# A decoder layer on one core: the second group's projections moved into the first group's cross-attention end and third norm

## The reference

```python
x = x + attn(layernorm(x))            # linear attention with decay
x = x + xattn(layernorm(x), ctx)      # causal cross-attention, 16 heads
x = x + ffn(layernorm(x))             # 8 experts, top 2, plus a shared one

# attn
xx = shift(x) - x                     # the token before, minus this one
r, k, v = (x + xx*maa_r) @ Wr.T + br, (x + xx*maa_k) @ Wk.T + bk, (x + xx*maa_v) @ Wv.T + bv
g = silu((x + xx*maa_g) @ Wg.T + bg)
# per head: att = r @ k * decay matrix; y = att @ v (and a carried state)
y = groupnorm(y) * ln_g + ln_b
return (y * g) @ Wo.T + bo
# xattn
return softmax(causal(q @ k.T / 4)) @ v @ Wout.T
# ffn
combine = top-2 softmax weights of x @ router_w.T
return sum_e combine_e * ((silu(x @ w_gate_e) * (x @ w_up_e)) @ w_down_e) + sigmoid(x @ shared_gate_w) * shared
```

## Time and profile before

| | |
|---|---|
| three runs | 650.09, 653.31 (median), 655.36 us |
| profiled execution | 653.28 us, span 651.6 us |
| busy | PE 608.5 (93%), DVE 409.7 (63%), POOL 337.5 (52%), ACT 277.4 (43%) |

### The profile page before, as it was taken

One profiled execution on the slowest core, in us unless ns is written; L12 is line 12 of the kernel. 1 busy time (PEld: TensorE's weight loads), 2 busy tenths in 40 slices (PEclk: granted clock), 3 DMA queues, 4 the chain that ended last, 5 costly groups with the idle time before them and its releaser, 6 DMA issues.

```text
span 651.6 us, 15490 instructions
## 1 busy us (share of the span) xinstructions
PE 608.5 (93%) x6296; PEld 484.9 (74%) x6296; DVE 409.7 (63%) x840; ACT 277.4 (43%) x632; POOL 337.5 (52%) x456
## 2 busy tenths in 40 slices
PE   7987958699999999999999999998999999999996
PEld 6544546454888889854888888854798888899996
DVE  6797787859743755869753655879762655742120
ACT  4856322132335655351325555342325555343322
POOL 7674154014355666615355666524364566618666
PEclk9989998799999999999999999999999999999999
DMA  7921000002020112102021111102011112114220
GB/s 188 352 82 34 1 1 2 2 1 66 26 83 25 42 41 59 28 16 68 20 82 32 39 41 58 30 17 68 16 51 34 38 43 58 28 55 113 69 69 16
DMA packets 41824, 34.08 MB, mean 52 GB/s; under 512 B 9901, under 2 KB 41206, under 8 KB 41754
## 3 DMA queue, kind: packets, MB, share of 16 engines
q1 hardware_dynamic: 39850, 31.27, 17.2%
q10 hardware_dynamic: 1904, 1.84, 0.9%
HBM read 30.92 MB, written 2.17 MB: 51 GB/s over the span
## 4 chain that ended last, share of the span: by engine, by line
PE 36%; DVE 23%; POOL 17%; ACT 11%; issue 10%; DMA 2%; ACTq 0%; SPq 0%; POOLq 0%; DVEq 0%
PE bank L1014 7%; DVE A L1504 6%; DVE nm L1581 5%; POOL hb L620 4%; POOL A L695 3%; POOL hT_last L704 3%; PE bank L1196 3%; POOL hT L609 3%; ACT A L885 2%; PE bank L1123 2%; ACT L799 2%; PE bank L1011 2%; PE bank L1213 2%; PE bank L1112 2%; DVE hb L1479 2%
## 5 line engine op out<-in xcount | busy, mean ns | idle before, releaser
L609 POOL TENSOR_TENSOR hT<-hb,hT 128x256 fp32r<-128x256 f32 (+1 forms) x102 | 78.2, 767 | 73.0 <-ACT hT L768 73.0
L620 POOL TENSOR_TENSOR hb<-hb,cwb 128x256 f32<-128x256 f32 (+1 forms) x102 | 77.2, 757 | 71.1 <-DVE hb L1479 71.0
L1479 DVE TENSOR_TENSOR hb<-hb,bank 128x256 f32<-128x256 f32 (+1 forms) x102 | 42.7, 419 | 105.1 <-ACT hb L778 105.1
L768 ACT ACTIVATE hT<-hb 128x256 fp32r<-128x256 f32 (+1 forms) x102 | 42.4, 416 | 126.6 <-POOL hb L620 126.1
L1018 PE MATMUL bank<-xTf,wGh 128*128 128x256 f32 x272 | 82.9, 305 | 0.0
L1504 DVE TENSOR_TENSOR A<-bank,decay 128x512 f32<-128x512 f32 x128 | 77.4, 683 | 8.2 <-PE bank L1112 8.2
L1019 PE MATMUL bank<-xTf,wGh 128*128 128x256 f32 x272 | 76.7, 282 | 0.0
L1020 PE MATMUL bank<-xTf,wGl 128*128 128x256 f32 x272 | 76.6, 282 | 0.0
L1019 PE MATMUL bank<-xTf,wUh 128*128 128x256 f32 x256 | 72.2, 282 | 0.0
L1018 PE MATMUL bank<-xTf,wUh 128*128 128x256 f32 x256 | 72.1, 282 | 0.0
L1020 PE MATMUL bank<-xTf,wUl 128*128 128x256 f32 x256 | 72.0, 281 | 0.0
(11 more groups left out here) (221 smaller groups left out, 1424.3 us busy)
## 6 DMA issues: line engine op xcount, KB each, us to landing
cwb<-cw_rows SPq DMA_DIRECT2D x54, 128.0 KB, 2.9
A<-cw_rows SPq DMA_DIRECT2D x18, 128.0 KB, 3.4
A<-in_x SPq DMA_DIRECT2D x4, 512.0 KB, 4.1
res<-in_x SPq DMA_DIRECT2D x4, 512.0 KB, 4.4
out_x<-res SPq DMA_DIRECT2D x8, 256.0 KB, 2.4
rawG<-in_L_ffn_w_gate SPq DMA_DIRECT2D x2, 704.0 KB, 6.4
rawU<-in_L_ffn_w_up SPq DMA_DIRECT2D x2, 704.0 KB, 6.5
cwb<-cw_rows SPq DMA_DIRECT2D x12, 112.0 KB, 2.6
```

What stands on the lines that cost most here:

```text
L609: pool.tensor_tensor(hT[hr, c % 2, 1, :], hb[hr, c % 2, :], hT[hr, c % 2, 0, :].bitcast(F32), ALU.subtract).then_inc(h_lo, 1)
L620: pool.tensor_tensor(hb[hr, c % 2, :], hb[hr, c % 2, :], cwb[hr, c % CWS, :], ALU.mult).then_inc(h_scaled, 1)
L1479: tt(h, h, up_part(PS[5 + c % 2], n), ALU.mult).then_inc(gu_used, 1)
```

## The change

All of it is in group 0 and at the start of group 1.

- POOL: the low parts of pieces 0 to 2 stand behind the last receptance and not between receptances. The down pieces 4 to 7 are no longer shared between DVE and POOL; POOL does them whole, 4 and 5 at n5 (behind piece 3), 6 and 7 behind the masks of batch 3. The power for group 1's first norm stands behind the masks of batch 1, and the zeroed edge behind those of batch 2.
- DVE: no down pieces. Differences and the first two mixed inputs of group 1 stand before `attended(2)`, the next two behind `attended(3)`, the following two between statistics and application of the third norm.
- ACT: the copy of the turned input (`mixed_input(1)`) stands in the midst of the exponentials of batch 3; r and k are taken before the third norm, g in front of the router's exponential, with a load of the Exp table behind it.
- PE: the first norm of group 1 is turned before batch 2 is attended. `project` takes a list of halves: r before the output product of cross-attention, k and half of v behind it, the other half of v behind the third norm, g's halves around the router's transpose. r's halves go to banks 6 and 5. The transposes of the routing weights stand inside the first scores of group 1. 17 idle products in place of 22 before the second norm. The first half of the output product waits for three normalised batches and not four.

```diff
+        def r_bank(g, m):
+            return (6, 5)[m] if g == 1 else (4, 2)[m]
...
             if n < 7:
-                j0, j1 = FD[n - 4]
-                cut = j0 + 2 * (j1 - j0) // 3
-                w = slice(cut, j1) if pool_side else slice(j0, cut)
+                w = slice(*FD[n - 4])
...
-        LOW_AT = dict(n5=(1, 2, 3), x0a=(0, 4, 5), r2=(6, 7))
-        LOW_POOL_AT = dict(n5=(3,), x1c=(4,), x3c=(5, 6))
+        LOW_AT = dict(n5=(1, 2, 3), x0a=(0,))
+        LOW_POOL_AT = dict(n5=(3, 4, 5), x3c=(6, 7))
...
-                    elif g == 0 and u >= 5:
-                        split_low(u - 5)
-                if g == 0:
+                if g == 0:
+                    for n in range(3):
+                        split_low(n)
...
-                    if b == 0 and g + 1 < NG:
+                    if b == (0 if g else 1) and g + 1 < NG:
                         layer_rstd(0, g + 1)
-                    if b == GB - 1 and g + 1 < NG:
+                    if b == (GB - 1 if g else 2) and g + 1 < NG:
                         zero_edge(g + 1)
...
-                        exponentials(b + 1, range(4))
+                        exponentials(b + 1, (0, 1))
+                        if b == 2:
+                            mixed_input(1)
+                        exponentials(b + 1, (2, 3))
...
                 if g == 0:
-                    mixed_input(1)
+                    take_rk(1, 0)
+                    take_rk(1, 1)
...
-                if g + 1 < NG:
+                if g == 0:
+                    take_g(1)
+                    act.activation(spare, mhalf[:, 0:1], ACT.Exp).then_inc(exp_table, 1)
+                elif g + 1 < NG:
                     take_rk(g + 1, 1)
...
                         elif n == 5 and g:
+                            if g == 1:
+                                turn_routing(0)
                             pe.wait_ge(cwT_ready, g)
...
-                    idle_product(22, 7)
+                    idle_product(17, 7)
...
                         key_scores(b + 1)
+                        if b == 2:
+                            pe.wait_ge(p_exp, 12)
+                            turn_norm(0, 1, tokx, 2)
                         attend(b)
...
                 if g == 0:
-                    turn_norm(0, 1, tokx, 2)
+                    project(1, 0)
...
-                halves = 2 if g else 4
+                halves = 2 if g else 3
...
+                else:
+                    project(1, 1)
+                    project(1, 2, (0,))
                 turn_norm(2, g, tok2, 0)
...
+                else:
+                    project(1, 2, (1,))
...
-                if g + 1 < NG:
+                if g == 0:
+                    project(1, 3, (0,))
+                elif g + 1 < NG:
                     project(g + 1, 1)
...
-                if g + 1 < NG:
+                if g == 0:
+                    project(1, 3, (1,))
+                elif g + 1 < NG:
                     project(g + 1, 2)
                     project(g + 1, 3)
...
-                    layer_apply(0, g + 1, tokx, tokx)
-                    point(g, "x2a")
+                    layer_apply(0, 1, tokx, tokx)
+                    input_differences(1)
+                    mixed_input(1, 0)
+                    mixed_input(1, 1)
                     attended(2)
                     attended(3)
+                    mixed_input(1, 2)
+                    mixed_input(1, 3)
```

More of the change, by code:

```diff
@@ L1070, in point, with turn_routing @@
                         ffn_tick(g - 1, n)
+            def turn_routing(g):
+                pe.wait_ge(cw_ready, g + 1)
+                for b in range(GB):
+                    last = nc.tensor.transpose(PS[cw_bank(g)][0:E + 1, b * T:(b + 1) * T], cw[:, b, :], ident[:])
+                last.then_inc(cw_turned, 1)
             pe.wait_ge(ident_made, 1)
@@ L1344, in _ @@
                         gate_up(g, n)
[L1345 to L1351 removed]
+                if g:
+                    turn_routing(g)
+                else:
+                    pe.wait_ge(f_lo[0], len(FW))
+                    pe.wait_ge(f_lo[1], NFW)
             for n in range(4, AHEAD):
@@ L1678, in _ @@
                 if g + 1 < NG:
-                    for c in range(4, 8):
+                    for c in range(4 if g else 6, 8):
                         mixed_input(g + 1, c)
```

34 lines of the change are left out of this document (14 added, 20 removed).

## The result

The changed kernel took 659.31 us (median of 4 runs, 657.62 to 660.45) against 653.19 for the kernel before (4 runs, 650.09 to 655.36): ratio 1.0095, 95% interval 1.0048 to 1.0142. It is slower. Run again, against other runs of the kernel before (the fifth experiment), it gave 1.0128, 1.0095 to 1.0162. I had forecast no change that can be told, 654.0, and 647.3 to 658.5: the measured time lies above my range, near what my slower rival gave (660.2). The profiled execution took 659.61 us with a span of 657.9. All ratios in this document are those on record and not quotients of the two medians; that of experiment 8 leaves out the two slow ones of its ten runs (656.02 and 656.54 us), and the plain mean of all ten over that of the kernel before is 0.9987.

What follows compares the result with a forecast made beforehand. No engine was taken to bound the kernel; the chain passes between engines. +3.9 (second norm, both early gains included) - 3.1 - 0.1 gave +0.7 us, 654.0; own range 651.5 to 657, over all cases 647.3 to 658.5.

Steps and rivals of the forecast that it cites:

- rival 2: PE's new gaps bring half clock in attention, last half projection and decay products: 6.9 us slower, 660.2; chance 0.07.
- Split pieces behind the receptances: POOL, group 0: PE's wait for the last receptance goes, moved pieces cost nothing before the memsets; gain 1.0 us.
- Five idle products fewer: PE before the second norm: 17 idle products for 22 let the norm be turned earlier; gain 0.7 us.
- The queue at the second norm: DVE's and POOL's split pieces run one by one after X, the norm's last output; maxima 3.9 us later, early gains included.
- The first rival: Second norm: back-to-back DVE instructions go ahead of waiting POOL, first maxima at 79.6; 647.2 in all, chance 0.15.
- To the third maxima: First to third maxima: DVE pieces and the power leave, batch 1's masks come earlier; 16.4 instead of 19.5, gain 3.1 us.
- To the first decay product: Third maxima (m) to the second group's first decay product: new chain takes 44.7 instead of 44.8 us, gain 0.1.
- My own sign of being wrong: Router product to first decay product: prediction wrong if the routing takes much longer than 13 us.
- After it 32 of them follow at the same pace: Second group's decay products: after the first, 32 follow at the pace before the change, so its shift is the time's shift.

Runs made afterwards that it cites:

- the fifth experiment: The changed kernel itself, unaltered, run again against other runs of the kernel before on another chip: 660.02 us, ratio 1.0128.
- experiment 8: Changed kernel with POOL's pieces 4 and 5 behind batch 1's masks, router exponential before the Silu, last down pieces held until group 1's second mixed input: 651.37 us, 0.9968.
- experiment 10: Kernel before with two early edits alone, split pieces behind the receptances and 17 idle products for 22: 650.97 us, ratio 0.9986.
- experiment 1: Changed kernel with POOL's down pieces 4 and 5 moved from the second norm to behind the masks of batch 1: 653.22 us, ratio 1.0043.
- experiment 4: Kernel before with only the changed kernel's whole split pieces and their tables, POOL doing all down pieces: 655.68 us, ratio 1.0079.
- experiment 3: Changed kernel with 17 idle products on PE between the router's transpose and the last half projection: 657.96 us, ratio 1.0115.
- experiment 7: Changed kernel with 17 idle products in the routing, plus 9 before and 3 behind the turning of the routing weights: 656.87 us, ratio 1.0099.
- experiment 9: Kernel of experiment 8 plus idle products: 17 before the last half projection, 4 behind it, 3 behind the routing weights' turning: 648.30 us, ratio 0.9960.
- experiment 11: Kernel before, nothing moved, with 16 idle products behind cross-attention's output product, before the third norm is turned: 651.45 us, ratio 1.0015.
- experiment 6: Changed kernel with ACT's router exponential before the gate's Silu and no Exp table load behind it: 657.74 us, ratio 1.0104.
- experiment 12: Changed kernel with POOL's down pieces 6 and 7 held until group 1's second mixed input is made: 658.32 us, ratio 1.0132.

## Why the prediction was wrong

1. **Split pieces behind the receptances**, -1.0. The wait of PE went: the last 20 decay products of group 0 follow without a gap and the group norm starts 1.2 us earlier. But 0.7 of it was lost at once, on something I had costed at nothing: POOL's memsets, which had ended just before a DVE instruction that works from SBUF to SBUF, now met it. DVE in the changed kernel:

```profile
57.08 0.97 DVE L1550 TENSOR_SCALAR A<-A 128x128 int32<-128x128 int32 x1
...
58.08 0.23 DVE L1552 TENSOR_SCALAR A<-A 128x128 int32<-128x128 int32 x1
```

 The same kind of instruction took 0.97 and 0.23 us; the memsets run from 56.98 to 57.97 (POOL's first row above). In all eleven profiled executions with these pieces moved the first of the two takes 0.82 to 0.99 us beside the memsets, and in the three others 0.23. X came 0.5 us earlier (72.90) and not 1.0.

2. **Five idle products fewer**, -0.7. Measured 0.5 (7.87 to 7.34 in experiment 10).

3. **The queue at the second norm**, with both early gains +3.9. Right in mechanism, and measured +3.7: first maxima forecast at 85.15, measured 84.92; experiments 1 and 4 show it alone, both ways. That it fits to 0.2 us is partly luck: X came 0.5 later than forecast, and the queue took 12.0 from X instead of 12.75. The first rival (DVE keeps its turn) is out: DVE and POOL took turns. The row behind it, the receptance at 32.42 that came in only after several short DVE instructions, stays unexplained. The rule of the Trainium skill that I set against the change ("SBUF — State Buffer", section "Who interferes with whom": the second to issue blocks until the first is through) agrees with this case's trace: DVE's two pieces took 9.07 us, nearly the 3.2 of their own plus the 6.3 of POOL's two.

4. **To the third maxima**, -3.1. Here the sum failed first. The step said "with 2.0 I take it to stay at full level"; it looked at the idle time in front of the attention and not at the 5.6 us that my own step 3 had just put in front of the key scores. PE ran at half clock from 84.9 to 98.6: measured -0.9, against a clock term of 0.8 that I had named and left out ("2.3 if the clock falls all the same"). With the maxima in time the section is 16.1 (experiment 1), near the 16.4 that I had worked out, so half clock costs 2.6 us here.

5. **To the first decay product**, -0.1. My chain gave 44.2 at full clock and 46.0 with half clock on the last half projection; I took 44.7. Measured 45.9, and 44.0 in the two kernels with idle products in the gap. The path was right, and the terms missed both ways. Up to the last of the 14 routing steps each came 0.7 to 1.2 us earlier than forecast: second mixed input m + 15.5 (16.5), router m + 30.6 (31.3), last of the steps m + 36.7 (37.6). From there to the end of the router's exponential it took 6.9 us and not 4.9, because of the half projection at half clock (3.78 instead of 1.85). The last steps took 2.3 and not 1.5, because of the receptance on POOL that I had costed at nothing. So the 44.0 of experiments 3 and 7, close to my 44.2, is luck: two errors of some 0.8 us cancel. My own sign of being wrong was a routing much longer than 13 us from the router product to the decay product, and it took 15.4 (134.13 to 149.48). (A slip without effect: PE's queue, 3 x 3.7 from m + 16.5 minus a quarter of a projection, is 26.7 and not 26.3, still in front of the norm.)

6. **"After it 32 of them follow at the same pace"**, the assumption at the head of the prediction. It is the step that failed by most: +2.7. I named the mechanism in rival 2 and gave it 7 in 100, as if the clock's terms were independent accidents. They belong together: my own timeline held the idle times, 5.5 and 4 us (measured 5.6 and 3.9), and the profile before had half clock at both of PE's longest idle times in that part: from 95.5 us, behind the 3.70 that ended at 95.01, and from 122.8, within the 4.04 that ended at 124.80. (It had a third stretch, from 109.1, with no idle time over 1 us ahead of it.) Rival 2's parts were: 1.5 in attention (measured 2.6 against experiment 1), 1.8 in the half projection (1.8 against experiment 3), 3.4 in the decay products (2.7). Its total, 660.2, lies near the 659.31 measured.

Whether the new order is worth anything by itself stays open. With the pieces in either of two other places it was still slower than the kernel before (1.0043 and 1.0080). With later pieces, the exponential first and the last pieces held it came level (experiment 8), and with idle products on top 0.4% ahead (experiment 9). The old order with idle products at its own waits was tried in one place only (experiment 11, 1.0015). What the runs do show is what spoilt it: where the split pieces were put, the two new waits of PE, and the gate with its table load in front of the router's exponential.

## What to carry to other kernels

When work is moved into an engine's gap, look for the gap that it leaves where it stood, and price PE's clock there by the nearest row in the same profile, as part of the likeliest case and not as a rival. The nearest row gives a size and no more: behind the same 3.88 us of idle time PE had from 3.4 us of half clock (experiment 6) to 17.1 (the changed kernel). Two long instructions with SBUF operands on DVE and POOL were one queue here: put POOL's beside DVE work that reads PSUM, where the same two pieces took 6.3 us instead of 9.0 and DVE's reciprocals their 1.76 (experiment 1). A short one counts too: one receptance beside a routing step cost 0.8 us. A table load and an activation in front of a small exponential that others wait for cost up to 2.9 us in the trace (experiment 6), which the timing does not resolve.

## What the runs showed of the hardware that I had not expected

The stretch at half clock was much longer than the idle time ahead of it: 13.7 us at the 5.2 to 5.6 us of idle time of the late maxima, in all seven profiled executions that have that wait (the changed kernel and experiments 3 to 7 and 12). At the 3.88 us of idle time in the routing it differed from one to the next: 17.1 us in the changed kernel, 3.4 and then 6.8 in its second profile, 3.4 in experiment 6; further waits follow there. In the one profiled execution of experiment 9, with idle products in the waits, PE was granted the full clock from 12.1 us to the end.

A POOL memset, which reads nothing, held up a DVE tensor_scalar from SBUF to SBUF (0.97 instead of 0.23 us in the changed kernel, 0.82 to 0.99 in eleven executions); its end at 58.04 follows that of the memsets at 57.97.
